# An attention block in float32: the low parts of q and k on GpSimd, q's factor in the exponential, a shorter chain of additions in the last halves

## The reference

```python
q = rmsnorm(q, gq, hd) * hd ** (-0.5)
k = rmsnorm(k, gk, hd)
attn = jax.nn.softmax(jnp.einsum('bhqd,bhkd->bhqk', q, k), axis=-1)
o = jnp.einsum('bhqk,bhkd->bhqd', attn, v)
```

## Time and profile before

| | before |
|---|---|
| median of three runs | 1813.49 us (1811.89 to 1816.94) |
| profiled execution, its own time | 1810.62 us |
| its span | 1808.8 us |
| mean granted TensorE clock | 0.987 |
| busy TensorE / VectorE / ScalarE / GpSimd | 1727.9 / 1085.6 / 919.6 / 372.5 us |
| attention loop, first exponential to last | 69.6 to 977.3 us |
| waits of the exponentials for scores | 178.7 us in 156 places |

### The profile page before, as it was taken

How to read it: one execution, slowest core, us unless ns; L and a number is a source line. 1 busy time by engine, 2 the same in 40 slices (tenths; PEclk the granted TensorE clock), 3 DMA queues, 4 the chain that set the end, 5 groups by cost and what they waited for, 6 DMA issues and landing times.

```text
span 1808.8 us, 23247 instructions
## 1 busy us (share of the span) xinstructions
PE 1727.9 (96%) x8376; PEld 1154.5 (64%) x8376; DVE 1085.6 (60%) x1325; ACT 919.6 (51%) x1136; POOL 372.5 (21%) x305
## 2 busy tenths in 40 slices
PE   6998999999999999999889999999999999999998
PEld 3554555555555555554224787878788887878786
DVE  6678888898898898878788545142332324142301
ACT  4476666777777777778787432222221212221221
POOL 3001111100001000000140233333332333333332
PEclk8999999999999999999999899999999999999999
DMA  5754545555555555555765201010020202010000
GB/s 195 214 144 132 135 123 139 132 147 135 154 135 134 146 130 156 127 135 153 174 144 196 74 18 58 25 52 24 12 70 6 64 17 64 17 52 23 17 18 24
DMA packets 122242, 176.92 MB, mean 98 GB/s; under 512 B 29568, under 2 KB 43904, under 8 KB 121136
## 3 DMA queue, kind: packets, MB, share of 16 engines
q1 hardware_dynamic: 115952, 156.41, 32.3%
q10 hardware_dynamic: 5408, 16.81, 2.5%
q0 software_dynamic: 800, 2.62, 0.5%
HBM read 124.87 MB, written 50.92 MB: 97 GB/s over the span
## 4 chain that ended last, share of the span: by engine, by line
PE 44%; issue 29%; DVE 11%; POOL 9%; ACT 4%; DMA 2%; SPq 0%; POOLq 0%; ACTq 0%; DVEq 0%
PE scores L513 9%; PE pv L530 8%; PE gemm L588 7%; DVE sums L791 5%; PE scores L1303 5%; POOL act_parts L1235 5%; PE gemm L601 4%; ACT probs L704 3%; PE pv L1320 3%; PE gemm L1320 2%; PE aux L554 2%; POOL y L1233 2%; PE aux L547 1%; DVE raw L816 1%; DVE raw L862 1%
## 5 line engine op out<-in xcount | busy, mean ns | idle before, releaser
L704 ACT ACTIVATE probs<-scores,shift 128x1024 f32<-128x1024 f32 x512 | 548.7, 1113 | 195.4 <-PE scores L513 178.7
L791 DVE TENSOR_TENSOR sums<-sums,probs 128x2048 f32<-128x2048 f32 x192 | 453.8, 2363 | 32.7 <-ACT probs L704 28.0
L513 PE MATMUL scores<-q_stack,k_stack 128*128 128x512 f32 x1024 | 358.8, 435 | 6.3 <-ACT probs L704 6.1
L1303 PE MATMUL scores<-w_hi,act_parts 128*128 128x512 f32 x1024 | 318.7, 392 | 0.0
L513 PEld LDWEIGHTS scores<-q_stack,k_stack 128*128 128x128 f32 x1024 | 173.8, 189 | 202.3 <-issue 105.5
L1235 POOL TENSOR_TENSOR act_parts<-act_full,act_parts 128x512 fp32r<-128x512 f32 x128 | 172.5, 1348 | 514.2 <-ACT act_parts L1166 513.6
L530 PE MATMUL pv<-probs,v 128*32 128x512 f32 x2048 | 253.1, 603 | 0.4 <-ACT probs L704 0.4
L1303 PEld LDWEIGHTS scores<-w_hi,act_parts 128*128 128x128 f32 x1024 | 191.4, 189 | 38.8
L1303 PE MATMUL scores<-w_lo,act_parts 128*128 128x512 f32 x512 | 199.9, 391 | 0.0
L1373 DVE TENSOR_TENSOR y_next<-pv,p_bias 128x512 f32<-128x512 f32 x28 | 19.3, 691 | 299.7 <-PE pv L1275 299.7
L1166 ACT ACTIVATE act_parts<-act_full 128x512 fp32r<-128x512 f32 x128 | 80.9, 632 | 224.5 <-PE scores L1303 223.5
(11 more groups left out here) (167 smaller groups left out, 1944.1 us busy)
## 6 DMA issues: line engine op xcount, KB each, us to landing
k_stack<-parts_scratch SPq DMA_DIRECT2D x128, 256.0 KB, 5.0
q_stack<-parts_scratch SPq DMA_DIRECT2D x128, 256.0 KB, 5.1
parts_scratch<-parts SPq DMA_DIRECT2D x62, 512.0 KB, 2.9
inverse<-inverse_scratch SPq DMA_DIRECT2D x128, 64.0 KB, 2.1
heads_out<-o_out SPq DMA_DIRECT2D x32, 256.0 KB, 5.2
out<-result SPq DMA_DIRECT2D x32, 256.0 KB, 2.0
heads<-heads_out SPq DMA_DIRECT2D x28, 256.0 KB, 3.6
x_tile<-in_x SPq DMA_DIRECT2D x28, 256.0 KB, 2.8
```

What stands on the lines that cost most here:

```text
L513: mm = nc.tensor.matmul(scores[p][:, i, :], k_stack[s][:, h, j * P:(j + 1) * P], q_stack[half][:, h, :], start=True, stop=True)
L704: nc.scalar.activation(probs[L % RING][:, 2 * p:2 * p + 2, :], scores[p][:], ACT.Exp, bias=small["shift"][:]).then_inc(exp_done, 1)
L791: nc.vector.tensor_tensor(sums[:], a[:], probs[l % RING][:], ALU.add).then_inc(added, 1)
L1303: mm = nc.tensor.matmul(acc[t], act_parts[m % 2][:, b, t * P:(t + 1) * P], w2[a][:, m, :], start=(m == 0 and i == 0), stop=(m == NM - 1 an ...
```

## The change

Three things change, all in the attention loop.

1. For units 4 to 63 the low part is no longer VectorE's: GpSimd subtracts the high part (`part_low`, at the same step, ahead of its other work of that step) once `part_hi` is signalled. Both parts are made without the factor of q.
2. The factor is the `scale` of the exponential, a value per partition read from SBUF, where before there was none.
3. `LEAN` = 26: from half 26 on VectorE leaves out the addition of the eighth tile. TensorE's row sum takes `sums` after the seventh tile and adds the eighth from `probs` with four more multiplications into the same bank. `adds_until` counts the additions; ScalarE waits for the row sum before it writes the eighth tile's buffer again.

```diff
--- before.py
+++ after.py
@@ -135,6 +135,15 @@
         step += 1
     SUM_AT[step] = n
 INV_AT, FIN_AT = ({step + after: n for step, n in SUM_AT.items()} for after in (1, 2))
+
+LEAN = -(-max(FILL) // NT)
+
+
+def adds_until(l):
+
+    hh, j = l // NT, l % NT
+    return ADDS * min(hh, LEAN) + (ADDS - 1) * max(0, hh - LEAN) + (min(j, ADDS - 1) if hh >= LEAN else j)
+
 
 STACK_LOAD = {}
 for step, n in FIN_AT.items():
@@ -541,10 +550,16 @@
                 pe.wait_ge(rows_moved, issued["rows"])
 
         def row_sums(hh):
-            pe.wait_ge(added, ADDS * (hh + 1))
+            pe.wait_ge(added, adds_until(NT * hh + NT - 1))
             aux_free()
             for h in range(HG):
-                mm = nc.tensor.matmul(aux[h * DH:(h + 1) * DH, :], small["ones"][:], sums[:, h, :], start=True, stop=True)
+                mm = nc.tensor.matmul(aux[h * DH:(h + 1) * DH, :], small["ones"][:], sums[:, h, :], start=True, stop=(hh < LEAN))
+            if hh >= LEAN:
+
+                l = NT * hh + NT - 1
+                pe.wait_ge(exp_done, 2 * l + 2)
+                for h in range(HG):
+                    mm = nc.tensor.matmul(aux[h * DH:(h + 1) * DH, :], small["ones"][:], probs[l % RING][:, h, :], start=False, stop=True)
             mm.then_inc(rs_mm, 1)
             issued["rows"] += 1
 
@@ -699,10 +714,12 @@
 
                 l = L - RING
                 act.wait_ge(pv_mm, l + 1)
-                act.wait_ge(added, ADDS * (l // NT) + max(1, l % NT))
+                act.wait_ge(added, adds_until(l + 1 if l % NT == 0 else l))
+                if l // NT >= LEAN and l % NT == NT - 1:
+                    act.wait_ge(rs_mm, l // NT + 1)
             act.wait_ge(qk_mm, 2 * L + p + 1)
             nc.scalar.activation(probs[L % RING][:, 2 * p:2 * p + 2, :], scores[p][:], ACT.Exp,
-                                 bias=small["shift"][:]).then_inc(exp_done, 1)
+                                 scale=small["s_gain"][:], bias=small["shift"][:]).then_inc(exp_done, 1)
 
         def move_rows(hh):
             act.wait_ge(rs_mm, hh + 1)
@@ -764,7 +781,13 @@
             pool.wait_ge(stat_clamped, n + 1)
             nc.gpsimd.tensor_tensor(x_inv[:, t:t + 1], x_sqc[:, t:t + 1], small["minus_half"][:, 0:1], ALU.pow).then_inc(inv_done, 1)
 
+        def part_low(n):
+            pool.wait_ge(part_hi, n + 1)
+            nc.gpsimd.tensor_tensor(parts_of(n)[:, 1, :], raw[n % 2][:], full(parts_of(n)[:, 0, :]), ALU.subtract).then_inc(part_lo, 1)
+
         for L in range(START, AFTER):
+            if L in FIN_AT and FIN_AT[L] >= 4:
+                part_low(FIN_AT[L])
             if L in SPLIT_AT:
                 split_h(SPLIT_AT[L])
             if L in STAT_AT:
@@ -777,7 +800,7 @@
 
         def add(l):
             j, hh = l % NT, l // NT
-            if j == 0:
+            if j == 0 or hh >= LEAN and j == NT - 1:
                 return
             dve.wait_ge(exp_done, 2 * l + 2)
             if j == 1:
@@ -786,7 +809,7 @@
                     dve.wait_ge(rs_mm, hh)
                 a = probs[(l - 1) % RING]
             else:
-                dve.wait_ge(added, hh * ADDS + j - 1)
+                dve.wait_ge(added, adds_until(l - 1))
                 a = sums
             nc.vector.tensor_tensor(sums[:], a[:], probs[l % RING][:], ALU.add).then_inc(added, 1)
 
@@ -867,10 +890,10 @@
                 elif n > 4:
                     dve.wait_ge(*stored(n - 1))
 
-            gain = small["s_gain"][:] if UNIT[n][2] == "q" else 1.0
-            nc.vector.tensor_scalar(parts_of(n)[:, 0, :], r[:], gain, None, ALU.mult).then_inc(part_hi, 1)
-            dve.wait_ge(part_hi, n + 1)
-            nc.vector.scalar_tensor_tensor(parts_of(n)[:, 1, :], r[:], gain, full(parts_of(n)[:, 0, :]), ALU.mult, ALU.subtract).then_inc(part_lo, 1)
+            nc.vector.tensor_scalar(parts_of(n)[:, 0, :], r[:], 1.0, None, ALU.mult).then_inc(part_hi, 1)
+            if n < 4:
+                dve.wait_ge(part_hi, n + 1)
+                nc.vector.tensor_tensor(parts_of(n)[:, 1, :], r[:], full(parts_of(n)[:, 0, :]), ALU.subtract).then_inc(part_lo, 1)
 
         setup["vector_first"](dve)
         for L in range(START, AFTER):
```

## The result

| | before | after |
|---|---|---|
| time, median of 12 runs each | 1811.8 us | 1819.2 us |
| ratio to before, 95% interval | | 1.0044, 1.0033 to 1.0054 |
| profiled execution: span | 1808.8 us | 1816.8 us |
| 208 steps with products (halves 0 to 25), first exponential to first | 778.6 us | 788.1 us |
| last six halves, to the last exponential | 127.9 us | 126.1 us |

The change costs 0.44%, 8.0 us (6.0 to 9.8): slower, as forecast, by a little less than the 9.5 forecast. (The forecast's 1823 us counts from 1813.5, the median of three runs; that of the twelve is 1811.8.) From here on a *half* is eight steps, counted from 0, and its length is the distance from its first exponential to that of the next half, which I took from the trace. In these terms the first stage is halves 0 to 6, the middle one 7 to 25 and the last 26 to 31.

A forecast was written before the change was run, and what follows sets the result against it. TensorE and VectorE were near their limit in the first and middle stages; a chain through exponentials and TensorE set the last stage's plain pairs. Terms -5.7 + 7.6 + 7.6 = +9.5 us on the median 1813.5 gave 1823, range 1807 to 1836.

The forecast's parts named there:

- lean row sums: Last six halves: TensorE sums the eighth tile, so two late row sums come in time; -5.7 us together.
- operand of the exponential: All 512 exponentials read a scale from memory, 80 ns more each where on the chain; +7.6 us, between 0 and 14.
- factor out of q's parts: The high part of q takes 427 ns instead of 487, some fifteen times on the chain; -0.9 us.
- low parts on GpSimd: Sixty subtractions move from VectorE, about 0.7 us each, to GpSimd, 1.29 us each; +8.5 us.
- The two costs of 0.84: Last stage: the longer row sum costs 0.84 us at each of the two boundaries that were on time.
- nine halves of the middle stage, 0.45 each, +4.0: Behind the high part, statistics and GpSimd's subtraction don't run beside each other, delaying the inverse root; +4.0 us.
- the stores of the parts come up to 2.9 us later, with steps to spare on SyncE before the loads that need them: SyncE's stores of the parts come later behind GpSimd's low parts, put at no cost.
- 3.6 + 2.9 - 2.0: First stage, low parts: ahead of moves needing them +3.6; statistics behind 2.5 and 0.4; unrelated moves sooner -2.0 us.
- relief reaching TensorE: Faster rival: GpSimd subtracts in VectorE's pauses, shortening TensorE's waits in first and middle stages; 1801 us, chance 0.14.
- the free operand: Rival: ScalarE reads the scale while the previous exponential runs, so 7.6 us go; 1815.5 us, chance 0.14.
- Worse, the queues behind: Slower rival: work queued behind GpSimd's parts, late stores, and moves and additions held at most units; 1835 us, chance 0.22.

The follow-up runs named there:

- b_lean4: The kernel before, with TensorE summing the eighth tile in halves 26, 27, 29 and 30 only; 1803.9 us, ratio 0.9961.
- e_imm: The changed kernel, with the exponential's scale an immediate number instead of a value read from memory; 1809.3 us, ratio 0.9991.
- b_lean2: The kernel before, with TensorE summing the eighth tile in halves 26 and 29 only; 1806.9 us, ratio 0.9969.
- b_scale: The kernel before, with only the factor moved from q's parts into the exponential, low parts staying on VectorE; 1815.0 us, ratio 1.0022.
- e_order2: The changed kernel, with SyncE's parts stores deferred behind the spread of the inverse, only from unit 29 on; 1816.0 us, ratio 1.0021.
- e_order: The changed kernel, with SyncE's parts stores deferred behind the spread of the inverse, unit 22 included; 1815.7 us, ratio 1.0019.
- e_first: The changed kernel, with low parts on GpSimd for units 4 to 23 only and on VectorE from unit 24; 1813.2 us, ratio 1.0016.
- e_lowdve: The changed kernel, with all low parts back on VectorE; 1811.5 us, ratio 1.0004.
- e_nolean: The changed kernel, with the eighth tile of the last six halves added on VectorE again; 1824.3 us, ratio 1.0070.

## Why the forecast held, and which of its steps did not

The sum was +9.5 us, the runs say +8.0. Term by term (us; runs: difference of two ratios times 1811, each uncertain by 2 to 3; profile: differences of halves). The lean row sums are those of the third part of the change, the eighth tile summed by TensorE:

| term | forecast | by the runs | by one profile |
|---|---|---|---|
| lean row sums | -5.7 | -4.7 | -5.8 |
| operand of the exponential | +7.6 | +9.6 | +8.7 |
| factor out of q's parts | -0.9 | -5.8 | -3.2 |
| low parts on GpSimd | +8.5 | +7.2 | +9.0 |
| sum | +9.5 | +6.3 | +8.7 |
| measured directly | | +8.0 | +8.0 (span) |

- **Row sums: right, to the pair.** Forecast 6.37 us for a pair without the dearer exponential; *b_lean4* has 6.40. Forecast 6.5 with it, and 6.58 measured. The two costs of 0.84 came as forecast (0.84 to 0.87 in halves 28 and 31 of *e_imm*, *b_lean2* and *b_lean4*). What I had not seen is that the set matters: a lean sum in 26 alone would have been paid back in 28.
- **Operand: right place, the size a little low.** 91 ns and not 80; the Trainium skill's figure (ScalarE: Activation LUTs, What ACT_TABLE_LOAD costs), about 93, is borne out, and its 8.8 us is the profile's 8.7. The last stage gave 3.5 (forecast 3.8). The middle one gave 4.5 (forecast 3.2); about 0.7 of the difference is the operand piling onto the late outputs of halves 10 and 18, which cost 2.0 with the low parts on GpSimd and 1.3 in *b_scale* (forecast 1.0).
- **Factor out of the parts: mis-sized.** I counted 60 ns "some fifteen times on the chain" and left out that the low part becomes a plain subtraction. The runs give 5.8 us with an interval from 3.6 to 8.0, and the profile 3.2, of which 2.6 lies in the stage that scatters by as much. So it is more than forecast; how much more stays open.
- **Low parts: the sum right, partly for the wrong reason.** The term "nine halves of the middle stage, 0.45 each, +4.0" failed: with SyncE's order mended (*e_order2*) the middle stage is 0.6 us longer than with the low parts on VectorE. The nine places cost 0.10 each against the low part on VectorE, 0.9 in all if every one counts in full, and 0.04 against the kernel before. The statistics begin 0.09 before the high part's record ends, and GpSimd, whose record begins 0.16 behind theirs, is done 1.14 us after their end and not 1.29 plus a signal; the inverse root ends 0.51 after that and not 0.61. In its place stands a cost that I put at nothing: "the stores of the parts come up to 2.9 us later, with steps to spare on SyncE before the loads that need them". I looked at who needs the data and not at who stands behind the store in the queue. It is 4.3 us in halves 10 and 18, and 4.2 to 4.5 by the runs of *e_order2* and *e_order*. That the term overrated and the one left out are nearly of one size is luck; without it the sum would have been 3 to 4 us further off.
- First stage: forecast 3.6 + 2.9 - 2.0 = 4.5, measured 2.2 by the runs (*e_first* against *e_lowdve*) and 3.4 by the halves of the changed kernel against *e_lowdve*; neither stands clear of its uncertainty. The waits answer to the earlier trace rows:

```profile
DVE raw L839 <- POOL parts L786: 18.3, 14, 1.5
PE gemm L603 <- DVE raw L839: 17.3, 14, 3.3
```

The move does wait for GpSimd's low part, 1.3 us in each of 14 places, and TensorE's wait for the move grows from 13.0 to 17.3 us (13.5 in *e_lowdve*), 4 more: the mechanism of the forecast and about its size. TensorE's waits for the moves of `v` shrink meanwhile from 3.9 to 2.0.

The rivals: relief reaching TensorE (1801) fell, since the kernel is 7.2 us faster with the low parts back on VectorE; the free operand fell with 91 ns. "Worse, the queues behind" named late stores among its reasons, but at the wrong place and size: the ordinary middle halves pay 0.15 each and not four times 0.16, and the first stage loses far less than 1 us at each of its 20 units.

## What to carry to other kernels

When an operation moves to a slower engine, list for each of its consumers what stands behind it in that consumer's queue. A store that nobody hurries for held a transfer that an output waited for. A wait removed at one boundary shortens the time that a fixed round trip has until the next one: compare the two before choosing where to apply the edit. And a smaller sum of busy time is not a shorter path: here GpSimd took VectorE's from 1085.6 to 1033.3 us, and the kernel became slower.

## What the runs showed of the hardware

- GpSimd's 60 subtractions fall into three kinds: 30 at 1.26 to 1.30 us (beside nothing, beside VectorE's moves from PSUM, or ahead of an addition that begins while they run), 23 at 1.64 to 1.68 and 7 at 3.26 to 3.36. The 30 of the last two kinds all stand behind a VectorE operation that reads SBUF twice and got in first (21 reductions, 2 subtractions, 7 additions), by 0.16 us as a rule, and they end 1.12 to 1.16 us after it: some 0.15 less than a subtraction takes alone.
- TensorE's granted clock in the last stage is 0.97 and 0.96 with the pauses of several microseconds before two row sums (before, *e_nolean*), 0.99 with one (*b_lean2*), and 1.00 without them (after, *b_lean4*).
- The first stage of the same instructions lasted 245.4, 242.4 and 244.7 us in three profiled executions (before, *b_lean2*, *b_lean4*), most of the difference in halves 3 and 5. Their first exponential began at 69.6, 70.7 and 72.5 us, also behind the same instructions. The first stage's halves from one execution each can't carry a claim of 2 us; those of the middle stage repeat within some 0.06 us.
